# Loops of the edge order, the permutation and the typed rows written out with static addresses

## The chip, the core and the metric

The kernel runs on one core of one Trainium2 chip. The metric is the device time of one execution in microseconds (us). PE is the matrix engine, PEld its weight loads, DVE the vector engine, ACT the scalar engine, POOL the GpSimd engine and SP the engine that issues most DMAs. "Sequencer" is the part of an engine that reads instructions, waits on semaphores and computes registers before it hands work to the engine proper.

## What is computed

Four graph layers run one after another on 3125 nodes of 256 features and 53125 edges. Each is followed by a residual sum and a row normalisation. Cut to what matters here:

```python
def reference(x, src, dst, edge_type_16, edge_weight, ...):
    # layer 0, three rounds: e = relu((x[dst]-x[src]) @ theta.T + x[src] @ phi.T)
    #                        agg = segment_max(e, src)        (edges grouped by SOURCE)
    # layer 1, two relational rounds:
    #   weight[r] = sum_b att[r, b] * basis[b]                (16 types, 8 bases)
    #   H[n, r]   = x[n] @ weight[r]
    #   agg       = segment_mean(H[src, type] * edge_weight, dst)   (edges grouped by TARGET)
    # layer 2: normalised sum over dst; layer 3: edge attention with 8 heads, then a feed-forward
    ...
```

The lists of edges arrive grouped by target. For layer 0 the kernel has to put them in the order of their sources itself. That sort is the first of the places that are changed. The second is the table `H` of the first relational round, which gives every node sixteen typed rows.

## The kernel before, in words

The edges stand in 128 x 416 slots (`STEPS` = 416 columns, 53125 edges and some padding). A column is handled as a tile of 128 edges. Eight tiles make a group (`GROUP` = 8), so there are 52 groups (`GROUPS`). Two sets of buffers and banks alternate, named by `h` = 0 and 1. A stage is a block in which each engine runs its own program. The engines meet only at semaphores, and all of them meet at the end of the stage.

**The edge order, `edge_order`, first stage ("stage A").** For each group DVE builds eight marked one-hot tiles `w` (`make_w`, L255). PE transposes them (L305) and counts with them (L309); both are `turn`. ACT copies the transposed tiles to `wt` (L341). PE multiplies each `wt` tile with itself (`compare`, L321). DVE keeps the counts (L263) and reduces the products to a rank within the tile (L272); both are `finish`. On DVE the order in one round of the loop is `make_w(2i)`, `finish(2i-1)`, `make_w(2i+1)`, `finish(2i)`. On PE it is `turn`, `compare`, `turn`, `compare`.

**Its third stage ("stage C").** For each group DVE adds the start of each node (`add`, L398), ACT rounds the sum to bf16 (`high`, L452), DVE forms the rest (`low`, L404), PE looks up eight tiles (`look_up`, L468), and DVE picks and sums (`pick` L411, `total_up` L419). One turn on DVE is `add(g+2)`, `low(g+1)`, `pick(g)`, `total_up(g-1)`.

**The permutation, `permute`.** It moves values to their place in the new order with products of one-hot tiles. DVE makes the one-hot tiles (L562, L565, L569), ACT weighs six of every eight of them (L589), and PE accumulates (L607). It runs with 104 groups of four tiles, and then a second time with 25 groups of one tile in which ACT has no part.

**The typed rows, `typed_rows`.** Eight chunks of two types, two chunks to a round of the loop. DVE mixes the weights of the next chunk (L2009, L2012), PE multiplies all 25 node tiles (L1964), ACT and DVE in turn copy the banks to ten staging buffers (L1984), and SP stores these to the table in DRAM (L1930).

In all of these, the first one or two groups are written out in Python with constant numbers, and the rest run in a hardware loop (`Fori`) whose index lives in a register. In the loop each address that depends on the index (`bass.ds(...)`) and each semaphore value to wait for (`wait_ge(copied, g - 1)`) is computed on the engine's sequencer. On PE and ACT each such wait is followed by an increment of a semaphore `held` that nobody waits for; it keeps the wait an instruction of its own. The loops of the edge passes, of the sort by target and of the attention pass are other functions and stay loops.

Of the kernel before, what the change touches and what calls it, by code (L numbers as in the profile page):

```python
# [25 lines left out]
P = 128  # L26
# [177 lines left out]
def edge_order(nc, env, order, target, given):  # L204
# [5 lines left out]
    with ExitStack() as stack:  # L210
# [10 lines left out]
        def tile_of(buffer, g, u, width):  # L221
            return buffer[:, bass.ds(g * (GROUP * width) + u * width, width)]
# [3 lines left out]
        with phase(nc, *names) as (hot, w_ready, turned, copied, counted, count_kept, compared, ranked, held, padded, loaded), \  # L226
# [22 lines left out]
            def _(dve):  # L249
                def make_w(g, h):  # L250
                    if later(g):
                        dve.wait_ge(counted, g - 1)
                    for u in range(GROUP):
# [3 lines left out]
                            scalar1=col_b[:, bass.ds(t, 1)], scalar2=col_a1[:, bass.ds(t, 1)],  # L257
# [3 lines left out]
                def finish(g, h):  # L261
                    dve.wait_ge(counted, g + 1)
                    nc.vector.tensor_tensor(  # L263
                        out=bulk(count[:, bass.ds(g * (GROUP * TILES), GROUP * TILES)], GROUP),
# [4 lines left out]
                    for u in range(GROUP):  # L269
# [3 lines left out]
                            out=products, in0=products, scalar=sq[:, bass.ds(t, 1)],  # L273
                            in1=env.after[:], op0=ALU.is_equal, op1=ALU.mult,
                            accum_out=rank[:, bass.ds(t, 1)])
# [18 lines left out]
            def _(pe):  # L294
                def turn(g, h):
                    pe.wait_ge(w_ready, g + 1)
                    pe.sem_inc(held, 1)
                    if later(g):
                        pe.wait_ge(copied, g - 1)
                        pe.sem_inc(held, 1)  # L300
                        pe.wait_ge(count_kept, g - 1)
                        pe.sem_inc(held, 1)
# [26 lines left out]
                with pe.Fori(1, GROUPS // 2) as i:  # L329
# [5 lines left out]
            def _(act):  # L335
                with act.Fori(0, GROUPS // 2) as i:
                    for h in range(2):
                        g = 2 * i + h
                        act.wait_ge(turned, g + 1)
                        act.sem_inc(held, 1)  # L340
                        nc.scalar.copy(wt[:, bass.ds(g * (GROUP * P), GROUP * P)], turn_bank[h][:, 0:GROUP * P]).then_inc(copied, 1)  # L341
# [37 lines left out]
        with ExitStack() as inner:  # L379
# [5 lines left out]
            with phase(nc, *names) as (added, cut_high, cut, looked_up, picked, placed, held), \  # L385
# [8 lines left out]
                def _(dve):  # L394
                    def add(g, h):
                        if later(g):
                            dve.wait_ge(cut, g - 1)
                        nc.vector.tensor_tensor(  # L398
                            out=part_of(h), in0=bulk(count[:, bass.ds(g * W1, W1)], GROUP),
# [7 lines left out]
                    def pick(g, h):  # L407
                        dve.wait_ge(looked_up, g + 1)
                        if later(g):
# [4 lines left out]
                            in1=bulk(hot_a[:, bass.ds(g * W1, W1)], GROUP).unsqueeze(2).broadcast_to([P, GROUP, 2, TILES]),  # L414
                            op=ALU.mult).then_inc(picked, 1)

                    def total_up(g, h):
                        dve.wait_ge(picked, g + 1)
                        nc.vector.tensor_reduce(out=place[:, bass.ds(g * GROUP, GROUP)], in_=bulk(found[:, h * W2:(h + 1) * W2], GROUP),  # L419
# [16 lines left out]
                    with dve.Fori(1, GROUPS // 2 - 1) as i:  # L436
# [8 lines left out]
                def _(act):  # L445
                    def high(g, h):
                        act.wait_ge(added, g + 1)
                        act.sem_inc(held, 1)
                        if later(g):
                            act.wait_ge(looked_up, g - 1)  # L450
                            act.sem_inc(held, 1)
# [3 lines left out]
                    with act.Fori(1, GROUPS // 2) as i:  # L455
# [4 lines left out]
                def _(pe):  # L460
                    def look_up(g, h):
                        pe.wait_ge(cut, g + 1)
                        pe.sem_inc(held, 1)
                        if later(g):
                            pe.wait_ge(picked, g - 1)
                            pe.sem_inc(held, 1)
# [7 lines left out]
                    with pe.Fori(1, GROUPS // 2) as i:  # L474
# [56 lines left out]
def permute(nc, env, blk, stp, pieces, tiles, group):  # L531
# [7 lines left out]
    def over_groups(engine, do):  # L539
# [3 lines left out]
        with engine.Fori(1, whole) as i:  # L543
# [5 lines left out]
    with ExitStack() as stack:  # L549
# [3 lines left out]
        with phase(nc, "hot", "marked", "used", "held") as (hot, marked, used, held), nc.Block() as block:  # L553
            @block.vector
            def _(dve):
                def make(g, h):
                    if not isinstance(g, int) or g >= RING:
                        dve.wait_ge(used, g - RING + 1)
                    for u in range(group):
# [3 lines left out]
                                                scalar1=stp[:, bass.ds(t, 1)], scalar2=None, op0=ALU.is_equal)  # L563
                        if u < by_act:
                            last = nc.vector.tensor_scalar(out=hot_block[:, v * P:(v + 1) * P], in0=env.iota_p[:],  # L565
                                                           scalar1=blk[:, bass.ds(t, 1)], scalar2=None, op0=ALU.is_equal)
                        else:
                            for i, piece in enumerate(pieces):
                                last = nc.vector.tensor_scalar(  # L569
                                    out=marked_piece[:, (v * n + i) * P:(v * n + i + 1) * P], in0=env.iota_p[:],  # L570
                                    scalar1=blk[:, bass.ds(t, 1)], scalar2=piece[:, bass.ds(t, 1)],
# [6 lines left out]
            def _(act):  # L578
# [3 lines left out]
                def mark(g, h):  # L582

                    act.wait_ge(hot, g + 1)
                    act.sem_inc(held, 1)
# [11 lines left out]
            def _(pe):  # L597
                def add(g, h, first=False, final=False):
                    pe.wait_ge(hot, g + 1)
                    if by_act:  # L600
                        pe.sem_inc(held, 1)
                        pe.wait_ge(marked, g + 1)
                    pe.sem_inc(held, 1)
# [11 lines left out]
                with pe.Fori(1, whole - 1) as i:  # L615
# [1265 lines left out]
def typed_rows(nc, env, y, turned_y, own, inverse, basis_dram, att_dram, root_dram, table):  # L1881
# [8 lines left out]
    with ExitStack() as stack:  # L1890
# [6 lines left out]
        with phase(nc, *names) as sems, nc.Block() as block:  # L1897
# [14 lines left out]
            def wait_read(engine, i, m):  # L1912

                if m >= 0:
                    engine.wait_ge((read_act, read_dve)[m % 2], i * reads + m // 2 + 1)
                    engine.sem_inc(held, 1)
# [1896 lines left out]
```

## Time and profile before

| | |
|---|---|
| median of 3 runs | 6430.61 us (6429.56 to 6430.99) |
| profiled execution, its span | 7532.0 us, 17.1% over the median |
| PE, DVE, ACT, POOL busy in it | 3093.3, 3776.4, 1789.8, 3184.4 us |
| stage A, profiled | from 47.6 to 280.2 us |
| stage C, profiled | from 313.7 to 405.6 us |
| permutation, its two runs, profiled | from 418.2 to 618.0 and from 621.1 to 632.7 us |
| typed rows, products, profiled | from 3308.4 to 3674.4 us, start of the last |

The profile is one execution, of which only the span is given; it is longer than those that were timed. Busy times in the rows below are unions, so that instructions which overlap on one engine count once. The spacing between the starts of two instructions is therefore often less than the duration shown for one.

### The profile page before, as it was taken

Reading aid. Unit: us, or ns where it says so; the run is one execution under the profiler, and the core shown is the slowest. Engines: PE = TensorE matmul, PEld = TensorE weight load, DVE = VectorE, ACT = ScalarE, POOL = GpSimd, SP = SyncE. Lnnn points to the kernel's source line nnn. Section 1 sums busy time; section 2 is a strip of 40 time slices with the busy share of each in tenths; the row PEclk is TensorE's granted clock in tenths of the full one; section 3 lists DMA queues with packets and bytes.
Section 4 is the critical chain, followed back from the end, with each engine's and each line's share of the span. In section 5 each row is a group of like instructions: output and inputs, shape, how many; then the busy total and the mean of one; then the engine's idle time right before and its main releaser. Section 6 shows DMA issues by size and latency. Waiting matters only on the chain. (4 is left out here: it accounts for less than half of the span.)

```text
span 7532.0 us, 76440 instructions
## 1 busy us (share of the span) xinstructions
PE 3093.3 (41%) x12803; PEld 1810.4 (24%) x12803; DVE 3776.4 (50%) x9366; ACT 1789.8 (24%) x4594; POOL 3184.4 (42%) x3188
## 2 busy tenths in 40 slices
PE   4474000433335455579500089200120016677648
PEld 3332000311113222244200044000110013555425
DVE  8995444444445555544455342333543344555553
ACT  1173000111111455421122221222210002222212
POOL 0002666334442656400366510566446654444440
PEclk9997555655556677789755599655555558888869
DMA  0002454323332444323455543455434545777730
GB/s 7 0 0 93 148 173 168 119 91 134 134 134 88 147 150 159 131 93 153 142 170 192 176 149 140 145 174 174 144 127 167 185 152 166 255 253 250 255 98 18
DMA packets 379735, 1064.44 MB, mean 141 GB/s; under 512 B 74258, under 2 KB 162612, under 8 KB 333012
## 3 DMA queue, kind: packets, MB, share of 16 engines
q1 hardware_dynamic: 213586, 595.68, 20.8%
q0 software_dynamic: 164688, 466.32, 20.8%
q8 instruction: 46, 0.75, 0.0%
q10 hardware_dynamic: 1330, 0.99, 0.0%
q14 instruction: 85, 0.70, 0.0%
HBM read 541.40 MB, written 521.29 MB: 141 GB/s over the span
## 5 line engine op out<-in xcount | busy, mean ns | idle before, releaser
L789 POOL DMA_INDIRECT out_of<-table,index x936 | 937.5, 1002 | 981.4 <-DVE index L813 710.8
L789 POOL DMA_INDIRECT rows<-table,index x728 | 725.7, 997 | 411.3 <-issue 229.2
L789 POOL DMA_INDIRECT rows<-typed_table,index x520 | 513.8, 988 | 638.1 <-DVE index L813 484.7
L3110 POOL DMA_INDIRECT qv<-qv_table,index x416 | 420.9, 1012 | 447.9 <-DVE index L3310 322.8
L789 POOL DMA_INDIRECT y<-typed_table,index x312 | 322.7, 1034 | 622.3 <-DVE index L813 531.5
L1494 PE MATMUL bank<-x,marks 128*128 128x416 f16 x1664 | 391.5, 401 | 366.4 <-ACT marks L1508 278.0
L828 DVE SCALAR_TENSOR_TENSOR y<-y,by_source_anew,out_of 128x256 f32<-128x256 f32 x897 | 433.9, 484 | 159.5 <-issue 32.2
L1508 ACT ACTIVATE marks<-hot_block,x 128x128 f16<-128x128 f16 x1248 | 371.6, 387 | 393.2 <-DVE marks L1549 362.5
L2163 PE MATMUL bank<-weights,turned_y 128*128 128x512 f32 x800 | 357.5, 596 | 5.5 <-ACT turned_y L2223 5.5
L3187 PE MATMUL bank<-weighed_rows,hot 128*128 128x272 f32 x832 | 283.8, 467 | 176.8 <-ACT y L3285 93.2
L1964 PE MATMUL bank<-weights,out_of 128*128 128x512 f32 x800 | 349.7, 595 | 13.2 <-DVE weights L2012 13.2
L807 ACT ACTIVATE rows<-rows,by_target_weight 128x256 f32<-128x256 f32 x520 | 215.8, 495 | 560.6 <-DMA rows<-typed_table,index 512.7
L3327 DVE TENSOR_TENSOR qv<-qv,bank 128x512 f32<-128x512 f32 x208 | 141.5, 684 | 362.6 <-PE bank L3175 165.1
L1494 PEld LDWEIGHTS bank<-x,marks 128*128 128x128 f16 x1664 | 182.5, 112 | 575.3 <-issue 492.7
L3175 PE MATMUL bank<-near,y 128*128 128x256 f32 x832 | 259.4, 454 | 143.5 <-DMA near<-k_rows 98.6
L828 DVE SCALAR_TENSOR_TENSOR state<-state,by_target_keep,rows 128x256 f32<-128x256 f32 x273 | 132.5, 485 | 282.1 <-issue 197.6
L2168 PE MATMUL bank<-ident,tail 128*128 128x128 f32 x2 | 0.7, 434 | 657.7 <-PEq L74 657.7
L3285 ACT COPY y<-bank 128x272 f32<-128x272 f32 x416 | 154.1, 387 | 479.3 <-PE bank L3187 193.4
L2426 PE MATMUL bank<-ident,tail 128*128 128x128 f32 x2 | 0.7, 434 | 643.5 <-PEq L74 643.5
L1628 POOL MEMSET floor<- 128x256 f32 x1 | 0.3, 312 | 615.8 <-POOLq L74 615.8
L828 DVE SCALAR_TENSOR_TENSOR y<-y,by_target_keep,rows 128x256 f32<-128x256 f32 x299 | 145.2, 486 | 222.0 <-issue 173.9
L828 DVE SCALAR_TENSOR_TENSOR out_of<-out_of,by_target_keep,y 128x256 f32<-128x256 f32 x299 | 145.0, 485 | 197.4 <-issue 112.7
(586 smaller groups left out, 7684.4 us busy)
## 6 DMA issues: line engine op xcount, KB each, us to landing
states<-y SPq DMA_DIRECT2D x156, 1024.0 KB
typed_table<-staged SPq DMA_DIRECT2D x400, 256.0 KB, 2.0
states<-state SPq DMA_DIRECT2D x78, 1024.0 KB
states<-out_of SPq DMA_DIRECT2D x78, 1024.0 KB
wide_states<-y SPq DMA_DIRECT2D x52, 1088.0 KB
near<-k_rows SPq DMA_DIRECT2D x416, 128.0 KB
out_of<-table,index POOLq DMA_INDIRECT x936
rows<-table,index POOLq DMA_INDIRECT x728
```

Source lines behind the costliest of these rows:

```text
L789: pool.indirect_dma_start(out=rows[h][:, u * D:(u + 1) * D], out_offset=None, in_=table, in_offset=bass.IndirectOffsetOnAxis(ap=index[h][: ...
L807: nc.scalar.activation(row, row, ACT.Copy, scale=order.weight[:, bass.ds((RING * i + h) * GROUP + u, 1)]).then_inc(weighed, 1)
L828: nc.vector.scalar_tensor_tensor(out=state[h][:, u * D:(u + 1) * D], in0=before, scalar=marks[:, bass.ds(g * GROUP + u, 1)], in1=rows[h][: ...
L1494: last = nc.tensor.matmul(env.bank[i][:, 0:STEPS], self.marks[h][i][:, u * P:(u + 1) * P], self.hot_step[h][:, u * STEPS:(u + 1) * STEPS], ...
L1508: last = nc.scalar.activation(self.marks[h][i][:, u * P:(u + 1) * P], self.hot_block[h][:, u * P:(u + 1) * P], ACT.Copy, scale=self.pieces ...
L1964: last = nc.tensor.matmul(bank[:, 0:pair], turned_y[:, a * D + s * P:a * D + (s + 1) * P], weights[h][:, s * pair:(s + 1) * pair], start=s ...
L2163: last = nc.tensor.matmul(products(m), turned_y[a % 2][:, s * P:(s + 1) * P], weights[:, c * 4 * D + s * pair:c * 4 * D + (s + 1) * pair], ...
L3110: pool.indirect_dma_start(out=qv[b][:, u * PAIR:(u + 1) * PAIR], out_offset=None, in_=qv_table, in_offset=bass.IndirectOffsetOnAxis(ap=ind ...
L3175: last = nc.tensor.matmul(env.bank[k % 2][:, j * D:(j + 1) * D], hot_turned[h][:, u * P:(u + 1) * P], near[h][:, u * D:(u + 1) * D], start ...
L3187: nc.tensor.matmul(env.bank[2 + j][:, 0:ROW], hot[b % RING][:, u * P:(u + 1) * P], weighed_rows[b % 2][:, u * ROW:(u + 1) * ROW], start=Tr ...
L3285: nc.scalar.copy(staged[h][:, u * ROW:(u + 1) * ROW], env.bank[2 + u % 2][:, 0:ROW]).then_inc(kept, 1)
L3327: nc.vector.tensor_tensor(out=q, in0=q, in1=by_step(env.bank[k % 2][:], D, 2), op=ALU.mult).then_inc(multiplied, 1)
```

## The change

Every `Fori` of these functions becomes a Python loop, so each round is written out. All addresses and all awaited values become constants, and the increments of `held` are dropped. The work, its order on each engine, the buffers and the semaphores that order the engines stay as they are. The other loops of the kernel are not touched.

```diff
+def span(at, width):
+    return slice(at, at + width)
...
         def tile_of(buffer, g, u, width):
-            return buffer[:, bass.ds(g * (GROUP * width) + u * width, width)]
+            return buffer[:, span(g * (GROUP * width) + u * width, width)]
...
                         last = nc.vector.tensor_scalar(
                             out=w[:, (h * GROUP + u) * P:(h * GROUP + u + 1) * P], in0=env.iota_p[:],
-                            scalar1=col_b[:, bass.ds(t, 1)], scalar2=col_a1[:, bass.ds(t, 1)],
+                            scalar1=col_b[:, span(t, 1)], scalar2=col_a1[:, span(t, 1)],
                             op0=ALU.is_equal, op1=ALU.mult)
...
-                with dve.Fori(1, GROUPS // 2) as i:
+                for i in range(1, GROUPS // 2):
                     make_w(2 * i, 0)
                     finish(2 * i - 1, 1)
...
                 def turn(g, h):
                     pe.wait_ge(w_ready, g + 1)
-                    pe.sem_inc(held, 1)
                     if later(g):
                         pe.wait_ge(copied, g - 1)
-                        pe.sem_inc(held, 1)
                         pe.wait_ge(count_kept, g - 1)
-                        pe.sem_inc(held, 1)
...
                 def compare(g, h):
                     pe.wait_ge(copied, g + 1)
-                    pe.sem_inc(held, 1)
                     if later(g):
                         pe.wait_ge(ranked, g - 1)
-                        pe.sem_inc(held, 1)
...
-                with pe.Fori(1, GROUPS // 2) as i:
+                for i in range(1, GROUPS // 2):
                     for h in range(2):
                         turn(2 * i + h, h)
                         compare(2 * i + h, h)
...
-                    with dve.Fori(1, GROUPS // 2 - 1) as i:
+                    for i in range(1, GROUPS // 2 - 1):
                         for h in range(2):
                             turn(2 * i + h, h)
...
                     def look_up(g, h):
                         pe.wait_ge(cut, g + 1)
-                        pe.sem_inc(held, 1)
                         if later(g):
                             pe.wait_ge(picked, g - 1)
-                            pe.sem_inc(held, 1)
...
         for h in range(RING):
             do(h, h)
-        with engine.Fori(1, whole) as i:
+        for i in range(1, whole):
             for h in range(RING):
                 do(RING * i + h, h)
...
                             last = nc.scalar.activation(
                                 marked_piece[:, (v * n + i) * P:(v * n + i + 1) * P], hot_block[:, v * P:(v + 1) * P],
-                                ACT.Copy, scale=piece[:, bass.ds(g * group + u, 1)])
+                                ACT.Copy, scale=piece[:, span(g * group + u, 1)])
...
             def over_pairs(engine, body):
 
                 body(0)
-                with engine.Fori(1, last_pair) as i:
+                for i in range(1, last_pair):
                     body(i)
                 body(last_pair)
...
-                            sp.dma_start(rows_of[a][:, bass.ds((2 * i + h) * pair, pair)], staged[m % slots][:]).then_inc(stored[m % slots], 16)
-                with sp.Fori(0, chunks // 2) as i:
+                            sp.dma_start(rows_of[a][:, span((2 * i + h) * pair, pair)], staged[m % slots][:]).then_inc(stored[m % slots], 16)
+                for i in range(0, chunks // 2):
                     body(i)
...
                     if k == 0 and (not isinstance(c, int) or c >= 2):
                         dve.wait_ge(filled, (c - 1) * TILES)
-                        dve.sem_inc(held, 1)
```

The same edits are made to the other addresses, loops and waits of these functions.

## Rows read from the trace of the kernel before

**Rows 1.** The profile's page: span, busy time, tenths of 40 slices.
```profile
span 7532.0 us, 76440 instructions
PE 3093.3 (41%) x12803; PEld 1810.4 (24%) x12803; DVE 3776.4 (50%) x9366; ACT 1789.8 (24%) x4594; POOL 3184.4 (42%) x3188
...
DVE  8995444444445555544455342333543344555553
```

**Rows 2.** Windows, the loops of stages A and C, the permutation, typed rows.
```profile
core 0: us, PE busy (x) PEld busy (x) DVE busy (x) ACT busy (x) POOL busy (x), PEclk, DMA share, GB/s
55.18:276.01 220.83, 125.50 (x1200) 100.98 (x1200) 213.64 (x1251) 50.43 (x50) 0.00 (x0) 1.00 0.01 2
317.64:398.29 80.65, 51.24 (x370) 38.29 (x369) 71.53 (x186) 17.04 (x46) 0.00 (x0) 1.00 0.00 0
420.06:612.23 192.17, 159.46 (x808) 72.07 (x808) 192.17 (x920) 189.40 (x612) 0.00 (x0) 1.00 0.00 0
3350.00:3600.00 250.00, 250.00 (x583) 110.58 (x582) 110.51 (x169) 42.79 (x73) 0.00 (x0) 1.00 0.39 153
```

**Rows 3.** Waits, stage A (engine, line, releaser: total us, times, longest).
```profile
DVE bank L272 <- PE bank L321: 10.1, 26, 1.6
```

**Rows 4.** Timeline, stage A, DVE: start, us, instruction [idle before, releaser].
```profile
55.18 1.87 DVE L255 TENSOR_SCALAR w<-iota_p,col_b,col_a 128x128 bf16<-128x128 bf16 x8
...
59.41 1.87 DVE L255 TENSOR_SCALAR w<-iota_p,col_b,col_a 128x128 bf16<-128x128 bf16 x8
...
276.01 0.36 DVE L263 TENSOR_TENSOR count<-bank,inv_a 128x200 f32<-128x200 f32 x1
...
277.93 0.36 DVE L272 SCALAR_TENSOR_TENSOR bank<-bank,tmp,after 128x128 f32<-128x128 f32 x1 [1.56 <-PE bank L321]
```

**Rows 5.** Timeline, stage A, PE's weight loads: constant addresses, then in the loop.
```profile
49.55 0.78 PEld L305 LDWEIGHTS bank<-ident,w 128*128 128x128 bf16 x8 [40.80 <-issue]
...
51.92 0.78 PEld L321 LDWEIGHTS bank<-wt 128*128 128x128 bf16 x8 [1.22 <-issue]
...
52.65 0.90 PEld L305 LDWEIGHTS bank<-ident,w 128*128 128x128 bf16 x8
...
157.54 1.07 PEld L321 LDWEIGHTS bank<-wt 128*128 x8 [1.52 <-issue]
```

**Rows 6.** Timeline, stage C: first rows constant addresses, the rest in the loop.
```profile
315.11 0.49 PE L468 MATMUL bank<-high_low,wt 128*128 128x50 bf16 x8 [3.00 <-DVE high_low L404]
...
317.64 0.36 DVE L398 TENSOR_TENSOR part<-count,by_source_start 128x200 f32<-128x200 f32 x1
...
319.63 0.35 DVE L398 TENSOR_TENSOR part<-count,by_source_start 128x200 f32<-128x200 f32 x1
319.90 0.36 DVE L404 TENSOR_TENSOR high_low<-part,high_low 128x200 bf16<-128x200 f32 x1
...
320.80 1.14 PE L468 MATMUL bank<-high_low,wt 128*128 128x50 bf16 x8 [0.98 <-DVE found L411]
321.14 0.35 DVE L398 TENSOR_TENSOR part<-count,by_source_start 128x200 f32<-128x200 f32 x1
...
322.17 0.57 DVE L411 TENSOR_TENSOR found<-bank,hot_a 128x400 f32<-128x400 f32 x1 [0.40 <-PE bank L468]
```

**Rows 7.** Timeline, end of stage C, after its loop.
```profile
401.80 0.36 DVE L404 TENSOR_TENSOR high_low<-part,high_low 128x200 bf16<-128x200 f32 x1
402.63 0.57 DVE L411 TENSOR_TENSOR found<-bank,hot_a 128x400 f32<-128x400 f32 x1 [0.48 <-PE bank L468]
```

**Rows 8.** Timeline, permutation, DVE: two at constant addresses, two in the loop.
```profile
420.06 0.32 DVE L562 TENSOR_SCALAR hot_step<-iota_steps,stp 128x416 bf16<-128x416 f16 x1
...
421.94 0.32 DVE L562 TENSOR_SCALAR hot_step<-iota_steps,stp 128x416 bf16<-128x416 f16 x1
...
606.57 0.33 DVE L562 TENSOR_SCALAR hot_step<-iota_steps,stp 128x416 bf16<-128x416 f16 x1
...
608.46 0.33 DVE L562 TENSOR_SCALAR hot_step<-iota_steps,stp 128x416 bf16<-128x416 f16 x1
```

**Rows 9.** DMA, 4360 to 4740 us: instruction queues (packets, MB, share).
```profile
q8 instruction: 8, 0.13, 0.1%
q14 instruction: 7, 0.06, 0.0%
```

**Rows 10.** Windows, the same stretch, which is straight-line code.
```profile
4360.00:4740.00 380.00, 367.82 (x953) 176.27 (x952) 131.32 (x264) 79.90 (x150) 4.12 (x5) 0.99 0.36 136
```

More of the change, by code:

```diff
@@ L263, in finish @@
                     nc.vector.tensor_tensor(
-                        out=bulk(count[:, bass.ds(g * (GROUP * TILES), GROUP * TILES)], GROUP),
+                        out=bulk(count[:, span(g * (GROUP * TILES), GROUP * TILES)], GROUP),
                         in0=bulk(count_bank[h][:, 0:GROUP * TILES], GROUP),
@@ L272, in finish @@
                         last = nc.vector.scalar_tensor_tensor(
-                            out=products, in0=products, scalar=sq[:, bass.ds(t, 1)],
+                            out=products, in0=products, scalar=sq[:, span(t, 1)],
                             in1=env.after[:], op0=ALU.is_equal, op1=ALU.mult,
-                            accum_out=rank[:, bass.ds(t, 1)])
+                            accum_out=rank[:, span(t, 1)])
                     last.then_inc(ranked, 1)
@@ L335, in _ @@
             def _(act):
-                with act.Fori(0, GROUPS // 2) as i:
+                for i in range(0, GROUPS // 2):
                     for h in range(2):
@@ L339, in _ @@
                         act.wait_ge(turned, g + 1)
-                        act.sem_inc(held, 1)
-                        nc.scalar.copy(wt[:, bass.ds(g * (GROUP * P), GROUP * P)], turn_bank[h][:, 0:GROUP * P]).then_inc(copied, 1)
+                        nc.scalar.copy(wt[:, span(g * (GROUP * P), GROUP * P)], turn_bank[h][:, 0:GROUP * P]).then_inc(copied, 1)
         ring.close()
@@ L398, in add @@
                         nc.vector.tensor_tensor(
-                            out=part_of(h), in0=bulk(count[:, bass.ds(g * W1, W1)], GROUP),
+                            out=part_of(h), in0=bulk(count[:, span(g * W1, W1)], GROUP),
                             in1=base[:].unsqueeze(1).broadcast_to([P, GROUP, TILES]), op=ALU.add).then_inc(added, 1)
@@ L413, in pick @@
                             in0=env.bank[h][:, 0:W2].rearrange("p (u s a) -> p u s a", u=GROUP, s=2),
-                            in1=bulk(hot_a[:, bass.ds(g * W1, W1)], GROUP).unsqueeze(2).broadcast_to([P, GROUP, 2, TILES]),
+                            in1=bulk(hot_a[:, span(g * W1, W1)], GROUP).unsqueeze(2).broadcast_to([P, GROUP, 2, TILES]),
                             op=ALU.mult).then_inc(picked, 1)
@@ L418, in total_up @@
                         dve.wait_ge(picked, g + 1)
-                        nc.vector.tensor_reduce(out=place[:, bass.ds(g * GROUP, GROUP)], in_=bulk(found[:, h * W2:(h + 1) * W2], GROUP),
+                        nc.vector.tensor_reduce(out=place[:, span(g * GROUP, GROUP)], in_=bulk(found[:, h * W2:(h + 1) * W2], GROUP),
                                                 axis=AX.X, op=ALU.add).then_inc(placed, 1)
@@ L454, in _ @@
                         high(g, g)
-                    with act.Fori(1, GROUPS // 2) as i:
+                    for i in range(1, GROUPS // 2):
                         for h in range(2):
@@ L473, in _ @@
                         look_up(g, g)
-                    with pe.Fori(1, GROUPS // 2) as i:
+                    for i in range(1, GROUPS // 2):
                         for h in range(2):
@@ L570, in make @@
                                     out=marked_piece[:, (v * n + i) * P:(v * n + i + 1) * P], in0=env.iota_p[:],
-                                    scalar1=blk[:, bass.ds(t, 1)], scalar2=piece[:, bass.ds(t, 1)],
+                                    scalar1=blk[:, span(t, 1)], scalar2=piece[:, span(t, 1)],
                                     op0=ALU.is_equal, op1=ALU.mult)
@@ L584, in mark @@
                     act.wait_ge(hot, g + 1)
-                    act.sem_inc(held, 1)
                     for u in range(by_act):
@@ L614, in _ @@
                     add(h, h, first=h == 0)
-                with pe.Fori(1, whole - 1) as i:
+                for i in range(1, whole - 1):
                     for h in range(RING):
@@ L1915, in wait_read @@
                     engine.wait_ge((read_act, read_dve)[m % 2], i * reads + m // 2 + 1)
-                    engine.sem_inc(held, 1)
             @block.sync
@@ L1951, in body @@
                         pe.wait_ge(mixed, (2 * i + h + 1) * (2 * BASES))
-                        pe.sem_inc(held, 1)
                         for a in range(TILES):
@@ L2003, in mix @@
                         dve.wait_ge(filled, (c - 1) * TILES)
-                        dve.sem_inc(held, 1)
                     w_r = weights[h][:].rearrange("p (s o) -> p s o", s=2)[:, :, r * D:(r + 1) * D]
                     basis_b = basis[:, b * 2 * D:(b + 1) * 2 * D].rearrange("p (s o) -> p s o", s=2)
-                    factor = att[:, bass.ds(c * (2 * BASES) + r * BASES + b, 1)]
+                    factor = att[:, span(c * (2 * BASES) + r * BASES + b, 1)]
                     if b == 0:
```

10 lines of the change are left out of this document (2 added, 8 removed).

## The prediction

> **What bounds the kernel now.** I read the page first, then the windows of the four changed places, then waits and timelines inside them. The page shows a span of 7532.0 us in which no engine is busy for more than half of the time, so the kernel is a sequence of stages with different limits, and an average says nothing about this change [rows 1]. The first slices of DVE read 8, 9, 9: the sort at the start is a DVE stage. The windows say the same per stage. In the loop of stage A DVE is busy for 213.64 of 220.83 us, in the loop of stage C for 71.53 of 80.65, in the permutation for 192.17 of 192.17, and in the typed rows PE is busy for 250.00 of 250.00 [rows 2]. A stage whose bounding engine is already full gains nothing from cheaper address arithmetic on a sequencer. So the change can only give back the time in which the bounding engine stands still, and that is small: the reader should see about 7 us missing in A, 9 us in C, and none in the other two.
>
> **Stage A.** The waits name one cause of idle DVE: the rank step L272 waits for PE's product L321, 10.1 us in 26 waits, the longest 1.6 [rows 3]. I price it by pace and not by idle time, because an instruction that comes after a wait also loses its overlap with the one before. The 25 rounds of the loop run from 55.18 to 276.01, which is 220.83 / 25 = 8.83 us per round of two groups. A group in which DVE waits for nothing takes 59.41 - 55.18 = 4.23 us, so 8.46 per round [rows 4]. The difference is 0.37 per round, or 9.2 us over 25. Would the wait go? The cycle on PE is: turn a group, wait for ACT's copy, multiply, turn the next. At constant addresses, in the second cycle's start, it took 52.65 - 49.55 = 3.10 us. There the eight weight loads of L321 took 0.78 us, and in the loop 1.07 us [rows 5]. Since DVE waits for PE in the loop, PE's cycle there is the mean of 4.42 us (220.83 / 50), just over DVE's 4.23. Constants bring it well under, and then DVE is late next and sets 4.23. Behind the loop the last L272 waits 1.56 us [rows 4] for a product that is itself from the loop; of this 0.3 us is weight loads (1.07 - 0.78) and I take 0.6 for the two awaited values that are computed before it, together 0.9. Stage A gives 9.2 + 0.9 = 10.1 us. The bounds are 0 (the wait stays) and 10.1 plus the rest of that last wait, 10.8.
>
> DVE's own dynamic addresses cost nothing: its sequencer runs ahead of the engine, and eight `make_w` take 1.87 us in the first round and in later ones [rows 4]. If this cover were gone the price would show as idle DVE with no releaser, of which the waits list none.
>
> **Stage C.** The 24 rounds of its loop run from 317.64 to 401.80 [rows 6, 7], 84.16 / 24 = 3.51 us each. A turn without a wait takes 321.14 - 319.63 = 1.51, so a round could take 3.02. The chain that is too long: `low` starts at 319.90, PE's eight look-ups start 0.90 later and take 1.14, and `pick` starts at 322.17 after an idle 0.40. With constant addresses eight of these took 0.49 us instead of 1.14 [rows 6]. That alone (0.65) is more than the 0.49 per round that is lost. So DVE sets the pace: 0.487 x 24 = 11.7 us. Of the waits at the end of the stage, the one of 0.48 goes [rows 7] and I take 0.8 with the one that follows it, an estimate. Stage C gives 12.5 us. The bounds are 0 and 12.5.
>
> **Permutation.** DVE starts a group at 420.06 and the next at 421.94 with constants, 1.88 us; in the loop at 606.57 and 608.46, 1.89 us [rows 8]. ACT is nearly as full, 189.40 of 192.17 [rows 2]. I cost this edit at 0; DVE's work hides it. The second run, 25 groups on DVE in 11 us, has the same form. The bounds are 0 and 104 x 0.01 = 1 us.
>
> **Typed rows.** PE is busy for every microsecond of the window, 583 matmuls in 250.00 us, 0.43 us each at the full clock, while DVE has work for 110.51 and ACT for 42.79 [rows 2]. The waits and addresses that are removed on PE, ACT, DVE and SP are hidden behind PE's queue. The 150 more store instructions that stand written out for SP are the same stores as before, in the same order on the same queue. I take 0. Were PE's queue to run dry at a round's end, each of the few rounds could cost up to about 1 us, and the window excludes that.
>
> **What is added.** Code. Loops are re-read; straight code must be fetched. The straight stretch from 4360 to 4740 us fetches 8 blocks for PE, 0.13 MB, while PE executes 953 matmuls and 952 weight loads [rows 9, 10]. That is about 240 instructions and 16 KB to a block; the other queue has half that per block (0.06 MB in 7). Written out, PE gets about 48 x 50 more instructions in A, 48 x 17 in C, some 1700 in the permutation and 250 in the typed rows: 5200, or 21 blocks. DVE and ACT get about 2900, or 24 blocks of half the size. In that straight stretch PE is busy for 367.82 of 380.00 us, so even if all its idle time were fetching, a block would cost 12.2 / 8 = 1.5 us. PE's new code runs faster than that stretch, about 12 instructions per us in A against 5, a block in some 21 us. I take 0, since transfers of a few us fit into 21, and keep 0 to 1.5 us a block.
>
> The Trainium skill has a rule for this ("Runtime: NRT & Kernel Launch", section "Instruction fetch mechanics"): blocks of 256 instructions are fetched ahead while the present one runs, and the crossing is mostly hidden; a taken branch that leaves the two held blocks makes the engine wait for a fetch. By the first half of it the sum stays as it is. By the second half leaving the loops would gain more than my sum; the gap-free pace of DVE and PE over their loop ends gives no sign of such a stop here.
>
> **Sum.** 10.1 + 12.5 + 0 + 0 + 0 = 22.6 us out of the profiled 7532.0. That execution is 17.1% over the median of 6430.61, and nothing shows where the extra lies. If it lay evenly, the gain would be 22.6 / 1.171 = 19.3 us. If it lay in the DMA stages, it would be 22.6. I take 21: 6430.6 - 21 = 6410 us.
>
> **Rivals.**
> *No difference.* The gaps are small differences of two near-equal cycles: 4.42 against 4.23 on PE and DVE in A. If recording the profile makes each sequencer instruction a little slower, PE's cycle in an ordinary execution may already lie under 4.23, and stage A gives nothing. 22.6 - 10.1 = 12.5 us, 6418, which is 0.19%. With C's wait gone as well it is 6430. For it: the wait in A hangs on 0.19 us in a cycle with four or five sequencer waits. Against it: C hangs on 0.49 us and on matmuls that take twice as long. Chance 0.27.
> *Slower by fetching.* The engines wait for blocks of code in the written-out stages. At 1.5 us for each of PE's 21 blocks it costs 32 us: 6430.6 - 22.6 + 32 = 6440. It decides from 22.6 / 21 = 1.1 us a block, if DVE's and ACT's cost nothing, and from 0.5 if all 45 cost alike. For it: the sort has no other straight code of that density to prove that fetching keeps up. Against it: PE's nearly full straight stretch. Chance 0.09.
> *More than the sum.* In ordinary executions the round ends cost something the profile hides, or the ends of stages shorten too: 28 to 32 us, 6400. The full windows speak against it. Chance 0.04.
> The forecast itself, 16 to 24 us less, has 0.60.
>
> **How the numbers follow.** About 0.2%, 13 us, is what a measurement of this kernel tells from no change. The forecast and the last rival are faster by more: 0.64. No difference 0.27, slower 0.09. The likeliest case's own range is 6406 to 6415. The range is 6402 to 6431: it takes in the case without a gain and leaves out the fetching and most of the larger gain.
>
> **What would show it.** Right: in the profile after, L272's wait for L321 nearly gone, stage A's groups 4.23 us apart, stage C's turns 1.51, the eight look-ups in about half a microsecond; permutation still 1.88 per group, typed rows still 0.43 per matmul with PE full. The second rival would show as DVE or PE idle with no releaser at intervals of some 20 us while the instruction queues are busy. The forecast is wrong if PE's chain with ACT still exceeds DVE's work in A, or if the profiled gain is there and the timed one is not.

## The result, and the profile after

The changed kernel takes 6399.42 us, median of 4 runs (6395.84 to 6424.32), against 6430.8 us for the kernel before in the same series. The ratio is 0.9953 with a 95% interval of 0.9939 to 0.9967, so 21 to 39 us less. It is faster, as forecast, by 31 us between the medians where 21 were forecast, and the median lies 2.6 us under the low end of the stated range.

The profiled execution of the kernel after spans 6422.6 us, not 7532.0 (it is the longest of the four executions). The 7532.0 are no property of the kernel before: the kernel before, profiled again (run e4 below), spans 6432.8 us. The first profile of before came from an execution in which the edge passes ran slower. The stage times below, all from the sort, agree between the two profiles of before to 0.1 us.

The windows of the changed kernel, in the order of [rows 2]: loops' part of stage A, of stage C, permutation, typed rows.

```profile
core 0: us, PE busy (x) PEld busy (x) DVE busy (x) ACT busy (x) POOL busy (x), PEclk, DMA share, GB/s
55.00:265.00 210.00, 113.55 (x1191) 95.24 (x1192) 210.00 (x1241) 49.59 (x49) 0.00 (x0) 1.00 0.01 3
306.00:379.00 73.00, 24.91 (x388) 18.48 (x389) 73.00 (x194) 18.16 (x49) 0.00 (x0) 1.00 0.00 1
397.50:589.00 191.50, 159.67 (x807) 72.74 (x808) 191.40 (x916) 189.08 (x611) 0.00 (x0) 1.00 0.00 1
2733.00:2983.00 250.00, 250.00 (x584) 110.98 (x583) 110.33 (x169) 42.12 (x72) 0.00 (x0) 1.00 0.39 153
```

DVE now has work in every microsecond of the loops' parts of A and C (210.00 of 210.00, 73.00 of 73.00). The permutation and the typed rows look as before. In stage C PE's busy time fell to 24.91 us for 388 matmuls, where it was 51.24 for 370 [rows 2]: the same work at half the time. Within such a group of eight nothing but the weight addresses was computed, and with the increments of `held` put back at constant addresses (e12) the eight take 0.49 us.

In the kernel before, DVE waited for PE in A [rows 3] and, in C, for the look-ups:

```profile
DVE found L411 <- PE bank L468: 10.3, 26, 0.5
```

In the changed kernel the wait for the look-ups is gone. The two longest waits of DVE between 47 and 406 us are the entry into the stage between A and C, and what is left of the wait for the product:

```profile
DVE count L349 <- PEq L74: 1.9, 1, 1.9
DVE bank L276 <- PE bank L320: 1.8, 2, 1.3
```

Of the 26 waits for the product two are left, those of the first and of the last group, which were outside the loop before. The timeline of the changed kernel, end of stage A and a turn of stage C:

```profile
266.66 0.37 DVE L267 TENSOR_TENSOR count<-bank,inv_a 128x200 f32<-128x200 f32 x1
267.58 0.36 DVE L276 SCALAR_TENSOR_TENSOR bank<-bank,tmp,after 128x128 f32<-128x128 f32 x1 [0.56 <-PE bank L320]
...
307.13 0.35 DVE L396 TENSOR_TENSOR part<-count,by_source_start 128x200 f32<-128x200 f32 x1
307.40 0.36 DVE L402 TENSOR_TENSOR high_low<-part,high_low 128x200 bf16<-128x200 f32 x1
...
307.68 0.57 DVE L409 TENSOR_TENSOR found<-bank,hot_a 128x400 f32<-128x400 f32 x1
307.81 0.52 PE L462 MATMUL bank<-high_low,wt 128*128 128x50 bf16 x8 [1.00 <-DVE high_low L402]
308.16 0.56 DVE L417 TENSOR_REDUCE by_source_anew<-found 128x8 f32<-128x400 f32 x1
308.64 0.36 DVE L396 TENSOR_TENSOR part<-count,by_source_start 128x200 f32<-128x200 f32 x1
```

A turn of C is 308.64 - 307.13 = 1.51 us on every group. The look-ups follow the end of `low` by 0.05 us and take 0.52; in [rows 6] they came 0.54 after it and took 1.14. The last wait of stage A fell from 1.56 [rows 4] to 0.56 us.

Where the time went in stage A of the kernel before is seen in PE's transposes (L305) and products (L321):

```profile
216.75 1.01 PE L305 MATMUL bank<-ident,w 128*128 128x128 bf16 x8 [0.71 <-DVE count L263]
...
219.43 1.26 PE L321 MATMUL bank<-wt 128*128 x8 [1.42 <-ACT wt L341]
220.92 1.01 PE L305 MATMUL bank<-ident,w 128*128 128x128 bf16 x8 [0.24 <-issue]
...
225.56 1.01 PE L305 MATMUL bank<-ident,w 128*128 128x128 bf16 x8 [0.71 <-DVE count L263]
```

PE's two groups of a round are not alike: 4.17 us from 216.75 to 220.92, and 4.64 from there to 225.56. The difference of 0.47 us stands at the end of the loop, where PE's program jumps back. In every round from the second on, the first transposes behind the loop's end start 0.68 to 0.72 us after PE's previous product has ended, those in the middle of the round 0.20 to 0.25. The named releaser, the count at L263, had ended 0.4 us before. Nor is it DVE's tiles: with DVE alone written out (e8) they are ready 0.83 us ahead of these transposes in place of 0.72, and the 0.71 stays. Two groups without the loop's end would take 2 x 4.17 = 8.34 us, less than DVE's 8.46.

Code fetches between 40 and 640 us, first the kernel before, then after, from the DMA view of that stretch (packets, MB, share):

```profile
q8 instruction: 2, 0.03, 0.0%
q14 instruction: 5, 0.04, 0.0%
```
```profile
q8 instruction: 21, 0.34, 0.2%
q14 instruction: 28, 0.23, 0.1%
```

Nineteen blocks more on PE's queue and 23 on the other. (q8 carries PE's code: with PE alone written out in A and C it fetches 14 blocks up to 613 us, with DVE alone still 2. The other queue fetches 5 and 15.) DVE has no gap in the loops' parts of A and C all the while, and 0.1 us of 191.50 in the permutation's. The fetches cost nothing where they are made.

### The profile page after: what moved, and what is told of

Its sections match the earlier page's. It is cut to its first block and busy times, and to the rows that moved or that the text cites. A ratio compares the mean times of both kernels' runs of the same rounds, so it can differ in the third digit from the quotient of the medians.

```text
span 6422.6 us, 69578 instructions
## 1 busy us (share of the span) xinstructions
PE 2953.5 (46%) x12777; PEld 1746.7 (27%) x12803; DVE 3771.8 (59%) x9366; ACT 1778.0 (28%) x4594; POOL 3219.9 (50%) x3188
## 5 line engine op out<-in xcount | busy, mean ns | idle before, releaser
L780 POOL DMA_INDIRECT out_of<-table,index x936 | 963.2, 1029 | 449.9 <-issue 281.4
L3173 PE MATMUL bank<-weighed_rows,hot 128*128 128x272 f32 x832 | 239.2, 412 | 46.7 <-ACT y L3271 44.5
L819 DVE SCALAR_TENSOR_TENSOR out_of<-out_of,by_target_keep,rows 128x256 f32<-128x256 f32 x299 | 145.0, 485 | 171.3 <-ACT rows L798 138.7
L1108 PE MATMUL bank<-x,hot_b 128*128 128x25 bf16 x416 | 19.5, 183 | 450.3 <-DVE x L1043 450.3
```

Source lines behind the costliest of these rows:

```text
L780: pool.indirect_dma_start(out=rows[h][:, u * D:(u + 1) * D], out_offset=None, in_=table, in_offset=bass.IndirectOffsetOnAxis(ap=index[h][: ...
L819: nc.vector.scalar_tensor_tensor(out=state[h][:, u * D:(u + 1) * D], in0=before, scalar=marks[:, bass.ds(g * GROUP + u, 1)], in1=rows[h][: ...
L3173: nc.tensor.matmul(env.bank[2 + j][:, 0:ROW], hot[b % RING][:, u * P:(u + 1) * P], weighed_rows[b % 2][:, u * ROW:(u + 1) * ROW], start=Tr ...
```

## The experiments

One number is read from every profile: the start of the DVE instruction that writes `ident_v` (L634 of before), the fourth behind the permutations. It marks the end of the sort and comes before every edge pass. It stands at 636.09 us in the kernel before and at 636.15 in its second profile.

| run | what is written out | end of sort, us | earlier by | ratio, 95% interval |
|---|---|---|---|---|
| after | all | 613.02 | 23.1 | 0.9953 (0.9939 to 0.9967) |
| e1 | edge order | 612.83 | 23.3 | 0.9957 (0.9943 to 0.9971) |
| e2 | permutation | 635.86 | 0.2 | 0.9997 (0.9988 to 1.0006) |
| e3 | typed rows | 636.57 | -0.5 | 1.0003 (0.9993 to 1.0012) |
| e4 | nothing (before again) | 636.15 | -0.1 | 0.9998 (0.9989 to 1.0007) |
| e5 | stage A | 625.71 | 10.4 | 0.9964 (0.9931 to 0.9997) |
| e6 | stage C | 623.70 | 12.4 | 0.9959 (0.9942 to 0.9976) |
| e7 | PE's programs of A and C | 613.35 | 22.7 | 0.9943 (0.9918 to 0.9969) |
| e8 | DVE's programs of A and C | 631.55 | 4.5 | 0.9969 (0.9950 to 0.9989) |
| e16 | as e8 | 631.58 | 4.5 | 0.9997 (0.9986 to 1.0008) |
| e9 | all, again | 612.25 | 23.8 | 0.9962 (0.9945 to 0.9979) |
| e13 | all, third time | 612.24 | 23.9 | 0.9957 (0.9944 to 0.9971) |
| e10 | all, 22 us of work added | 634.75 | 1.3 | 0.9984 (0.9966 to 1.0003) |
| e14 | as e10 | 634.67 | 1.4 | 0.9990 (0.9977 to 1.0003) |
| e11 | nothing, 22 us added | 658.52 | -22.4 | 1.0025 (1.0004 to 1.0046) |
| e15 | as e11 | 658.77 | -22.7 | 1.0038 (1.0022 to 1.0055) |
| e12 | all, `held` kept on PE | 613.06 | 23.0 | 0.9965 (0.9947 to 0.9983) |
| e17 | nothing, PE's code shifted | 636.12 | 0.0 | profile alone |
| e18 | all, PE's code shifted | 612.48 | 23.6 | profile alone |

The series e5 to e8, e9 to e12 and e17 to e18 ran on chips on which the kernel before took 7643, 7519 and 7629 us. The intervals there are 26 to 50 us wide, so for these runs the profile has to decide. In one series the ratios do not fit it: e5, e6, e7 and e8 come out 28, 31, 44 and 24 us faster by ratio, where the sort ends 10.4, 12.4, 22.7 and 4.5 us earlier. The intervals of e6 (18 to 44 us), e7 (24 to 63) and e8 (8 to 38) leave out what the sort shows. The excess is 17 to 21 us in all four, whatever is written out, and the four share one set of runs of the kernel before. So it looks like an offset of that set. e16 bears this out for e8; for e5, e6 and e7 it was not tested.

**e1 to e4, one place at a time.** Each takes one function from the changed kernel: `edge_order`, `permute` or `typed_rows`.

```diff
-                with pe.Fori(1, GROUPS // 2) as i:
+                for i in range(1, GROUPS // 2):
...
-            return buffer[:, bass.ds(g * (GROUP * width) + u * width, width)]
+            return buffer[:, span(g * (GROUP * width) + u * width, width)]
```

> Only the edge order (stages A and C) is written out; the permutation and the typed rows keep their loops. Theory 1 (the gain is the two gaps of DVE in the order): 22 to 24 us less than the kernel before, A and C shorter by 10.4 and 12.4 us in the profile. Theory 2 (some of the 31 us come from the other two places, hidden in the profile): about 15 us less.

Measured: 6401.51 us against 6434.76, ratio 0.9957, and the sort ends 23.3 us earlier. The difference is in the edge order. The profile gives theory 1; the ratio, 19 to 37 us less, excludes the 15 us of theory 2.

> Only the two permutations are written out. Theory 1: no difference, within 2 us, a group of four tiles still 1.88 us. Theory 2: a part of the 8 us that my sum misses, so 3 to 8 us less.

Measured: ratio 0.9997, no difference, as theory 1 had it.

> Only the typed rows are written out. Theory 1: no difference, within 2 us, PE full at 0.43 us a matmul. Theory 2: a part of the missing 8 us, so 3 to 8 us less, by an earlier start or end of the stores on SP.

Measured: ratio 1.0003, no difference. The end of the sort lies before the typed rows and says nothing of them; their products take 366.0 us from the first start to the last in e3, as in the kernel before, and 365.9 in the changed one. Theory 2's share of these two places is excluded to about 8 us for the one and 5 us for the other.

> The kernel before, unchanged, as a comparison with itself and for a second profile of it. Ratio 1.000 within the interval; its spread tells how much of the 31 us can be scatter. The profiled span tells whether the 7532 us shown for it belong to the kernel (then about 7500 again) or to that one execution (then about 6450).

Measured: ratio 0.9998, profiled span 6432.8. What made the first profile 1100 us longer lies behind the sort, nearly all of it in the edge passes and the attention pass; the products of the typed rows take 366 us in both. It is seen in one stretch of the first edge pass, before in the first line and e4 in the second; the code is the same:

```profile
750.00:1000.00 250.00, 13.43 (x190) 8.46 (x190) 116.75 (x228) 5.85 (x22) 150.96 (x153) 0.50 0.45 151
```
```profile
750.00:1000.00 250.00, 17.76 (x253) 11.26 (x253) 152.46 (x300) 7.71 (x29) 191.46 (x193) 0.50 0.60 200
```

POOL issued 153 gathers in 250 us in one and 193 in the other, and the DMA engines moved 151 against 200 GB/s. The sort, which moves next to nothing (2 GB/s in the loop of A [rows 2]), took the same time in both. Why the gathers came more slowly was not found.

**e5 and e6, one stage each.**

> Only stage A of the edge order is written out. Theory 1: 10.4 us less, all of it inside stage A, a group 4.23 us. Theory 2 (leaving the loops also helps what runs after them): more than 15 us less, with a part that appears only after the sort.

> Only stage C is written out. Theory 1: 12.4 us less, a turn 1.51 us. Theory 2: more than 17 us less, again with a part after the sort.

Measured: the sort ends 10.4 and 12.4 us earlier. The sum is 22.8 us. That is theory 1 by the profile. The ratio of e6, 18 to 44 us, would speak for theory 2; it may carry the offset named under the table, and e6 was not repeated elsewhere.

**e7 and e8, one engine each.** In A and C only PE's loops are written out and only its `held` dropped, or only DVE's loops.

> In stages A and C only PE's program is written out; DVE and ACT keep loops, registers and computed waits. Theory 1 (PE's sequencer makes the gaps): the same 22 to 23 us less. Theory 3 (DVE's and ACT's own sequencers have a share): 10 to 18 us less.

> In stages A and C only DVE's program is written out; PE and ACT keep their loops. Theory 1: no difference within 2 us, L272 still waits for L321 about 10 us and L411 for L468 about 10 us. Theory 3: 5 us or more less.

Measured: PE alone gives 22.7 us, all of it. DVE alone gives 4.5 us, all in stage C, where its wait for the look-ups falls from 10.3 to 5.9 us; in stage A it gives nothing. The waits of e8 in stage C:

```profile
DVE found L415 <- PE bank L472: 5.9, 26, 0.5
```

The timeline of e8 shows where it comes from:

```profile
340.31 1.14 PE L472 MATMUL bank<-high_low,wt 128*128 128x50 bf16 x8 [0.79 <-DVE found L415]
...
341.48 0.58 DVE L415 TENSOR_TENSOR found<-bank,hot_a 128x400 f32<-128x400 f32 x1 [0.20 <-PE bank L472]
```

`pick` starts 0.03 us after the look-ups end (340.31 + 1.14 = 341.45); in [rows 6] it was 0.23 after (320.80 + 1.14 = 321.94, and 322.17). So DVE's own arithmetic did cost something there, against theory 1 and the prediction: behind a wait that is really waited for, something is still computed, the second awaited value of `pick` or its address; e8 does not part them. In stage A the same step shrank, from 0.14 us between product and L272 to 0.04 in every second group, but there it gives nothing: PE's rounds still take 8.81 us, with the same 0.71 and 0.24 us before the transposes. The 4.5 us are not additional, since PE's code alone already removes the wait. The ratio of e8, 0.9969, looked like 24 us for 4.5; the same kernel on a 6433 us chip (e16) gave 0.9997.

> Only DVE's programs of stages A and C written out, whose profile showed 4.4 us less in stage C. Theory A: ratio 0.9990 to 0.9997. Theory B (writing out helps behind the sort): 0.9985 or less.

**e12, waits as separate instructions.** The increments of `held` come back on PE, at constants:

```diff
                     pe.wait_ge(w_ready, g + 1)
+                    pe.sem_inc(held, 1)
```

> The changed kernel with PE's increments of held in stages A and C kept, so that each wait stays an instruction of its own before the work it guards, at constants. Theory 1 (what cost the time were computed addresses, which double the pace of PE's matmuls in C, and computed values): the sort still shorter by 22 us or more. Theory 4 (the separate wait instructions were the cost): 10 us or more of it lost, L272 and L411 waiting again.

Measured: the sort ends 23.0 us earlier. Dropping the increments is worth at most 0.8 us beside e9 and nothing beside the first profile of after (613.02). In e12 the look-ups start later behind `low` than in the changed kernel, and nothing waits for them (timeline of e12):

```profile
340.96 0.36 DVE L407 TENSOR_TENSOR high_low<-part,high_low 128x200 bf16<-128x200 f32 x1
...
341.24 0.57 DVE L414 TENSOR_TENSOR found<-bank,hot_a 128x400 f32<-128x400 f32 x1
...
341.62 0.49 PE L469 MATMUL bank<-high_low,wt 128*128 128x50 bf16 x8 [1.02 <-DVE high_low L407]
```

**e9, e13 and the padded kernels.** The ratio 0.9953 is 30 us, the sort gives 23. Is the rest a gain behind the sort? The padded kernels compute `hot_a` three times, which costs back what the sort gained and keeps all else:

```diff
                 nc.vector.tensor_tensor(
                     out=bulk(hot_a[:], STEPS), in0=col_a1[:].unsqueeze(2).broadcast_to([P, STEPS, TILES]),
                     in1=env.iota_a1[:].unsqueeze(1).broadcast_to([P, STEPS, TILES]), op=ALU.is_equal).then_inc(hot, 1)
+                dve.wait_ge(hot, 2)
+                nc.vector.tensor_tensor(  # the same once more, and again
...
```

> The changed kernel once more, unchanged. 22.8 us are located in the sort. Theory A (the rest of the 31 us is scatter of the stages with edge passes): ratio about 0.9965. Theory B (leaving the loops also gives 5 to 9 us behind the sort): ratio about 0.9953 again.

> The changed kernel with the tensor hot_a (L279) computed three times in place of once, about 22.1 us more work on DVE in stage A, which gives back what the sort gained and starts all later stages at the old time. Theory A: ratio 1.000 to the kernel before. Theory B: about 0.999 (6 to 8 us less remain).

> The kernel before with the same two extra computations. Theory A: 22 us more, ratio 1.0034. Theory C (a shift of all later stages in time is worth more than itself, by how edge passes fall together with other transfers): 27 us or more, ratio 1.0042 or over.

> The changed kernel again. Theory A (22.8 us in the sort, the rest scatter): ratio 0.9962 to 0.9968. Theory B (5 to 9 us more behind the sort): 0.9950 to 0.9956.

> The changed kernel with hot_a computed three times, which costs back 22.1 us. Theory A: ratio 0.9995 to 1.0005. Theory B: 0.9986 to 0.9991.

> The kernel before with hot_a computed three times. Theory A: 22 us more, ratio 1.0031 to 1.0037. Theory C (a shift of the later stages is worth more than itself): 1.0042 or over.

Measured: e9 0.9962, e13 0.9957, e10 0.9984, e14 0.9990, e11 1.0025, e15 1.0038. The three measurements of the changed kernel (30, 29 and 28 us less) each hold 24 us in their interval and all lie above it; so do e1 (28) and e12 (26). The padded ones, 1.3 and 1.4 us ahead at the end of the sort, give 12 and 6 us less with intervals that hold zero. Of the values set beforehand, e9 came close to theory A's, e13 fell between the two, e14 within B's and e10 beyond B's; e16 is at the edge of A's. e11 costs 19 us for 22.4 and e15 24 for 22.7, so theory C has no support, though both intervals hold its 1.0042. Between A and B the ratios do not decide.

Nor do the profiles. On the 6430 us chips the time from `ident_v` to the start of the last DVE instruction is 5784.3, 5777.7, 5783.0, 5787.9 and 5765.9 us with the edge order in loops (e4, e2, e3, e16, e15) and 5773.5, 5797.2, 5781.7 and 5767.8 with it written out (e1, after, e13, e14). The means are 5780 and 5780, but single profiles differ by 31 us, so a gain of a few us could not be seen. One stretch of layer 0's third edge pass takes 408 to 410 us in six of these nine profiles and 399 to 401 in three (after, e14, e15), whichever the kernel. Single edge passes scatter by more than what is missing.

**e17 and e18, where a code fetch falls.** One difference behind the sort did repeat. The weights of the first rows (`load_relative`, L1604) are used 4.9 us after their load is issued in e4, and 3.6 us after in e1. In the first a code block of PE is fetched 1.2 us after the issue, in the second no block of PE is. It is so in all twenty profiles: 4.5 to 5.2 us where PE's queue fetches a block between issue and use, 3.4 to 3.6 where it does not. A block on the other queue alone (after, e9, e10, e12, e13, e14) leaves it at 3.4 to 3.5. The instruction queue in e4's DMA view from 653 to 658 us, which e1 and e17 lack there:

```profile
q8 instruction: 1, 0.02, 1.7%
```

Small matmuls that write an unread bank while PE waits for DVE move PE's code against its blocks:

```diff
+                    for _ in range(32):          # 48 in e18, on the changed kernel
+                        nc.tensor.matmul(env.bank[2][:, 0:TILES], env.after[:], env.ones[:, 0:TILES], start=True, stop=True)
                     pe.wait_ge(summed, 1)
```

> The kernel before with 32 small matmuls more on PE (128 instructions) while PE waits for DVE in the edge order's second stage; they write a bank nobody reads and hide behind that wait. If the 1.4 us at the first rows come from PE's code block being fetched together with the weights' load, the block is now fetched about half a block earlier and the weights arrive about 3.5 us after their issue in place of 4.9. If the cause is another, 4.5 to 5.2 us stay.

> The changed kernel with 48 such matmuls (192 instructions), which bring the next block's fetch forward to the time of the weights' load. If the fetch delays the load, the weights now arrive 4.5 to 5.2 us after their issue in place of 3.5. If not, 3.5 stays.

The timelines of e4, e17, e1 and e18, issue of the first of the two loads and first use:

```profile
653.04 0.40 SPq L1604 DMA_DIRECT2D weights<-in_L_gnn_thetas  x1
...
657.96 0.69 DVE L1660 TENSOR_TENSOR weights<-weights 128x512 f32<-128x512 f32 x1 [15.53 <-DMA weights<-in_L_gnn_phis]
```
```profile
653.00 0.40 SPq L1606 DMA_DIRECT2D weights<-in_L_gnn_thetas  x1
...
656.41 0.69 DVE L1662 TENSOR_TENSOR weights<-weights 128x512 f32<-128x512 f32 x1 [13.81 <-DMA weights<-in_L_gnn_phis]
```
```profile
629.83 0.40 SPq L1598 DMA_DIRECT2D weights<-in_L_gnn_thetas  x1
...
633.39 0.69 DVE L1654 TENSOR_TENSOR weights<-weights 128x512 f32<-128x512 f32 x1 [14.17 <-DMA weights<-in_L_gnn_phis]
```
```profile
630.02 0.40 SPq L1597 DMA_DIRECT2D weights<-in_L_gnn_thetas  x1
...
634.64 0.69 DVE L1653 TENSOR_TENSOR weights<-weights 128x512 f32<-128x512 f32 x1 [15.69 <-DMA weights<-in_L_gnn_phis]
```

The kernel before with its fetch moved away (to 15.9 us after the issue) uses the weights after 3.4 us in place of 4.9. The changed kernel with a fetch moved onto the load (1.0 us after the issue) uses them after 4.6 in place of 3.5. Both as expected if the fetch delays the load. So 1.1 to 1.5 us of the gain come from where the code happens to lie.

The lead grows a little more behind it. In the nine profiles on the 6430 us chips the weights' use comes 1.4 us sooner after `ident_v` with the edge order written out, on the mean. Thirty us after `ident_v`, at the copies of the first rows, it is 1.9 us, and 150 us after, in the first edge pass, 2.1 (149.0 to 150.9 us in the five with loops, 147.1 to 148.4 in the four without). What adds the 0.7 us was not tested. Farther on the scatter is larger than this.

## Why the prediction was right and wrong

**The mechanism was right for what it priced.** "The change can only give back the time in which the bounding engine stands still": e1, e2 and e3 put all that is located up to the end of the sort in the edge order, and e5 and e6 split it between its two stages. Both waits went, and both paces came out as stated: DVE full in A, 1.51 us per turn in C.

**The terms.** Stage A was 10.1 and measured 10.4; of this the last wait was taken at 0.9 and gave 1.0. Stage C was 12.5 and measured 12.4. The permutation was 0 and is 0.2 at the end of the sort, a point that moves by up to 0.8 without cause (-0.5 in e3, where nothing before it is changed; 613.02 and 612.24 in the changed kernel). The typed rows were 0, and their products take 366 us with and without the loops. The sum of 22.6 stands against 23.1 to 23.9 measured for all of the sort.

**The step that failed** is the rest of the sum, and what was done with it. "10.1 + 12.5 + 0 + 0 + 0" has no term for anything behind the sort. The profiles show a lead of 1.4 us more at the first rows, because a block of PE's code no longer falls onto their load, and of about 2.1 us by the middle of the first edge pass. Then the sum was made smaller: "If it lay evenly, the gain would be 22.6 / 1.171 = 19.3 us ... I take 21." The 17.1% by which the profiled execution exceeded the median did not touch the sort at all (636.09 and 636.15 us). It belonged to that execution, and scaling by it cost 1.6 us. On the sum, 22.6, the forecast would have been 6408, still 9 us above the measured median.

**What stays open.** With the lead behind the sort 25 to 26 us are located, and 31 were measured between the medians. By the five ratios of kernels with the edge order written out (after, e1, e9, e12, e13) the rest is 1 to 5 us. Each interval allows that it is scatter, and no profile shows a place for it; that it is nothing was not shown. The range's low end, 29 us under the median before, left little room for either.

**The rivals.** *No difference* was to keep C's 12.5 us at most, if the recording made stage A's wait. The timed difference of e1, 19 to 37 us, is more than that. *More than the sum*, with a chance of 0.04 and 28 to 32 us, has the measured 31 in it. Neither of its two reasons is borne out. The loop's end does cost time on PE, but in the profile and inside the 9.2 us of stage A. Ends of stages that shorten could make 0.3 to 1.1 us at most (23.1 to 23.9 for the sort against 22.8 for A and C). That its number came out was in part luck.

**PE's cycle in stage A** was taken as one value, the mean of 4.42 us, and the pace over the loop's end as free of gaps. It is 4.17 and 4.64 us in turn, and the 0.47 us between them stand at the loop's end. Without them PE's two groups (8.34 us) would be faster than DVE's (8.46), so the loop's end by itself may have made stage A's wait. A loop on PE with constant addresses was not built, and what the 0.47 us are, the branch or the values formed anew behind it, stays open. In stage C the loop's end hardly matters: the look-ups start 0.54 us after the end of `low` behind it [rows 6] and 0.49 in the middle of a round (from 342.81 to 343.30 us). There the addresses, 0.65 us for eight, and the awaited values are the cost.

**DVE's own addresses** "cost nothing": true in A by the time, where e8 gives nothing. In C they, or the second awaited value, made up to 4.5 us of the wait, hidden under PE's part, so the sum was not harmed. The sign that the prediction named, idle DVE without a releaser, could not show this: the cost stood inside a wait that had one.

**The rival by fetching** was wrong in the place it named. Counted at 21 and 24 blocks, 19 and 23 came, and DVE ran on without a gap. The rule of the Trainium skill ("Runtime: NRT & Kernel Launch", "Instruction fetch mechanics") that crossings are mostly hidden held there. Its other half, that a taken branch outside the two held blocks stops the engine, shows nowhere: PE's queue fetched 2 blocks between 40 and 640 us of the kernel before, in which PE jumped back 24 times in A alone. The 0.47 us at each of these are no fetch.

## What to carry to other kernels

Look first at who bounds a loop: computed addresses cost where the sequencer is on the chain (PE with small matmuls, one address each, 0.14 us against 0.06), and a little more behind a wait that is really waited for (0.23 us against 0.03); an engine that is full hides them. Look at each group of a round by itself: a mean of two hides what the loop's end costs. Price a wait by the pace of the loop with and without it, not by its idle time. When the profiled execution is longer than the timed ones, find the stage where the excess lies before scaling a sum by it. Where several variants share one set of comparison runs, an excess that is the same in all of them is no gain of any.

## What was not expected of the hardware

A 16 KB fetch of PE's code that starts about 1 us after two 256 KB loads are issued holds the use of the loaded weights back by 1.1 to 1.5 us (4.9 against 3.4 us, and 4.6 against 3.5). A change of code length in one stage can so move the time of another.

The end of a loop on PE costs 0.47 us a round in stage A (0.71 us before the transposes behind it, 0.24 before those in the middle), although no code is fetched.

The same kernel takes 6433 us in some series and 7519 to 7643 in others. Between the two profiles of before the difference lies nearly all in the edge passes and the attention pass (151 against 200 GB/s in one stretch), while the sort, which computes, ends within 0.1 us of the same time.
